# A transformer kernel on one core: seven products of zeros on TensorE at the start, and the splits of two weight blocks moved

## What is computed

```python
xn = _layernorm(x, axis=-1)
q = jnp.einsum('bsd,ed->bse', xn, Wq)
k = jnp.einsum('bsd,ed->bse', xn, Wk)
v = jnp.einsum('bsd,ed->bse', xn, Wv)
kvt = jnp.cumsum(k * v, axis=-2) * denom
vhat = q * kvt
x = x + jnp.einsum('bse,fe->bsf', vhat, Wo) + _L0_ffn_ref(xn, ...)
```

## Time and profile before

| | |
|---|---|
| three runs, us | 727.02, 727.24, 730.93 (median 727.24) |
| the profiled execution's own time, us | 730.96 |
| its span, us | 729.1 |
| mean granted clock of TensorE, share of full | 0.988 |
| TensorE matmuls busy | 667.8 us (92% of the span) |
| VectorE / ScalarE / GpSimd busy | 69% / 54% / 49% |

### The profile page before, as it was taken

How to read it: one execution, slowest core, us unless ns; L and a number is a source line. 1 busy time by engine, 2 the same in 40 slices (tenths; PEclk the granted TensorE clock), 3 DMA queues, 4 the chain that set the end, 5 groups by cost and what they waited for, 6 DMA issues and landing times.

```text
span 729.1 us, 13255 instructions
## 1 busy us (share of the span) xinstructions
PE 667.8 (92%) x4656; PEld 536.8 (74%) x4656; DVE 505.1 (69%) x964; ACT 395.1 (54%) x694; POOL 358.8 (49%) x299
## 2 busy tenths in 40 slices
PE   4998899899889899999899999989999989999996
PEld 4776676798878677776677777677777767777774
DVE  6978769568576748675867686585858486568645
ACT  3664325456455554754854482765475395448173
POOL 1346685766566533461646263454537162326453
PEclk9999899999999899999999999999999999999999
DMA  8437847697776577020025021004303000302100
GB/s 315 133 127 232 302 151 231 224 284 252 263 266 198 185 226 223 20 70 2 1 76 125 4 63 27 1 2 124 80 8 81 2 1 30 81 9 59 30 2 30
DMA packets 66804, 82.76 MB, mean 113 GB/s; under 512 B 7090, under 2 KB 50354, under 8 KB 66738
## 3 DMA queue, kind: packets, MB, share of 16 engines
q1 hardware_dynamic: 63156, 73.39, 31.8%
q0 software_dynamic: 3072, 8.39, 3.6%
q10 hardware_dynamic: 512, 0.13, 0.1%
HBM read 40.34 MB, written 28.84 MB: 95 GB/s over the span
## 4 chain that ended last, share of the span: by engine, by line
PE 52%; ACT 11%; DVE 11%; issue 10%; SPq 8%; DMA 4%; POOL 3%; ACTq 1%; POOLq 0%; DVEq 0%
PE acc L660 4%; SPq L623 4%; PE acc L662 4%; PE acc L661 4%; SPq L619 3%; PE pm L660 2%; PE pm L662 2%; PE ring L660 2%; PE pm L661 2%; PE ring L997 2%; PE ring L661 2%; PE ring L662 2%; PE pv L660 2%; POOL xs L1638 2%; ACT act L1490 2%
## 5 line engine op out<-in xcount | busy, mean ns | idle before, releaser
L1600 POOL TENSOR_TENSOR hl<-hf,hh 128x512 fp32r<-128x512 f32 (+1 forms) x76 | 100.5, 1322 | 230.1 <-ACT hh L1281 230.1
L1281 ACT ACTIVATE hh<-hf 128x512 fp32r<-128x512 f32 (+1 forms) x76 | 47.6, 629 | 75.4 <-DVE hf L2152 60.8
L660 PE MATMUL acc<-hh,wh 128*128 128x512 f32 (+1 forms) x168 | 70.4, 419 | 5.8 <-POOL hl L1600 5.8
L2216 DVE TENSOR_REDUCE mx<-ring 128x2 f32<-128x512 f32 (+1 forms) x96 | 61.6, 683 | 10.3 <-PE ring L999 10.3
L662 PE MATMUL acc<-hl,wh 128*128 128x512 f32 (+1 forms) x168 | 66.7, 397 | 0.0
L661 PE MATMUL acc<-hh,wl 128*128 128x512 f32 (+1 forms) x168 | 66.6, 396 | 0.0
L2152 DVE TENSOR_TENSOR hf<-hf,pv 128x512 f32<-128x512 f32 x64 | 43.6, 682 | 30.7 <-PE pv L662 29.3
L1739 POOL TENSOR_TENSOR pl<-act,ph 128x512 f16<-128x512 f32 x32 | 41.5, 1298 | 34.3 <-ACT ph L1495 31.4
L1472 ACT ACTIVATE hf<-pm 128x512 f32<-128x512 f32 x56 | 33.4, 596 | 44.6 <-PE pm L662 38.7
L1027 PE MATMUL ring<-qT,kT 98*128 98x256 bf16 (+1 forms) x256 | 43.8, 248 | 12.1 <-ACT act L1490 12.1
L660 PE MATMUL pv<-xh,wh 128*128 128x512 f32 x128 | 53.5, 418 | 0.0
(11 more groups left out here) (292 smaller groups left out, 2084.7 us busy)
## 6 DMA issues: line engine op xcount, KB each, us to landing
w4s<-w4hl SPq DMA_DIRECT2D x16, 512.0 KB, 4.2
ws<-qs SPq DMA_DIRECT2D x12, 512.0 KB, 5.2
qT<-qp SPq DMA_DIRECT2D x96, 64.0 KB
kT<-kp SPq DMA_DIRECT2D x96, 64.0 KB
xs<-yg SPq DMA_DIRECT2D x2, 2944.0 KB, 13.4
ys<-act SPq DMA_DIRECT2D x22, 256.0 KB, 3.7
stage<-w SPq DMA_DIRECT2D x8, 608.0 KB, 4.6
xh<-xs SPq DMA_DIRECT2D x12, 256.0 KB, 4.5
```

The source lines that it names most:

```text
L660: pe.matmul(o, w_hi, x_hi, start=first, stop=False, skip_group_check=True)
L1281: a.activation(h_parts(n)[0][0:rows, :], hf[0:rows, n % 2, :], ACT.Copy).then_inc(s_hh, 1)
L1600: return pool.tensor_tensor(dst, src, hi.bitcast(F32), ALU.subtract)
L2216: v.tensor_reduce(mx[:, i, h0:h0 + nh], ring[j % 2][:, :].rearrange("p (n k) -> p n k", n=nh), AX.X, ALU.max).then_inc(s_mx, 1)
```

## The change

TensorE gets seven products at the very start, after a wait for `s_zero`. Both operands are the zeroed tensor `yg`; each writes bank `ring[3]` (128 x 512), which nobody reads before `qkv(0,1,0)` overwrites it. On ScalarE the high parts of blocks 2 and 3 are made between `tokens_hi(0)` and `token_std(1)`; before, block 2 came behind `token_std(1)` and block 3 behind `v_scaled(0,1)`, together with block 4. GpSimd's and VectorE's own queues are as before; GpSimd's low part of block 3 waits for ScalarE's high part.

```diff
@@ constants
 EARLY, TURN_W = 13, 15
+WARM = 7
@@ TensorE
+            pe.wait_ge(s_zero, 1)
+            for _ in range(WARM):
+                pe.matmul(ring[3][:, :], yg[:, 0, 0:P], yg[:, :, :].rearrange("p a d -> p (a d)"), start=True, stop=True,
+                          skip_group_check=True)
             pe.wait_ge(s_ident, 16)
             turn_tokens(0)
@@ ScalarE
             token_std(0)
             weights(0, 1)
             tokens_hi(0)
+            weights(2, 3)
             token_std(1)
-            weights(2)
             for g in range(G):
                 v_scaled(g, 0)
                 if g < G - 1:
                     tokens_hi(g + 1)
                 v_scaled(g, 1)
                 if g == 0:
-                    weights(3, 4)
+                    weights(4)
```

## The result

| | before | after |
|---|---|---|
| median of 20 runs, us | 728.62 | 726.87 |
| lowest to highest, us | 725.68 to 732.38 | 722.53 to 730.12 |
| ratio to before, 95% interval | | 0.9969 (0.9954 to 0.9984) |
| span of the profiled execution, us | 729.1 | 723.3 |

The change makes the kernel faster by 0.31% of 728.6, 2.3 us, with 1.2 to 3.4 us in the interval; the medians differ by 1.75. The 0.5% of the prediction is not reached. The profiled executions differ by 5.8 us, more than the medians, so the span is no measure for the gain; what the rest is stands in "Why the prediction held".

A forecast was written before the change was run, and what follows sets the result against it. TensorE, busy 92% of the span, loses time at the start to the low clock and waits. VectorE's lead of 1.55 us, smaller than TensorE's 2.05, gives 727.24 - 1.55 = 725.7 us; range 723.4 to 729.6.

The forecast's parts named there:

- The smaller lead counts: After the first attention: of TensorE's lead of 2.05 us and VectorE's of 1.55, the gain is 1.55.
- The zeros: TensorE's start: seven zero products run from 1.35 us and end at 9.2, the clock rising after 3.7 us.
- What they delay: First tokens: transposes start 0.6 us later but run faster; `qkv(0,0,0)` stays at 11.2, its 18 products end at 15.4.
- GpSimd holds norm 1: Group 1's norm on VectorE: GpSimd's block 3 split, 12.9 to 15.3, makes it end at 16.4, 0.8 us later.
- The scans are freed: VectorE's scans in `attention(0,1)`: no longer held by GpSimd, they take 1.27 us and attention ends at 23.95, not 25.51.
- The whole gain is block 3's: At the start: moving block 3 brings the gain; the zeros bring about 0.2 us to VectorE's chain, nothing that decides.
- Rival 1: TensorE, 15.4 to 17.5: the clock falls without products, adding 1.7 us to the next ones; 727.1 us, chance 0.18.
- The rule against the zeros: TensorE, 9.2 to 11.2: transposes may not keep the clock up, so it may fall; sum the same within 0.5 us.
- Rival 2: TensorE's start: zeros outlast the tokens' arrival, each us beyond 9.2 delaying norm 1 by one; up to 729.9 us, chance 0.12.
- Rival 3: Group 1's norm: GpSimd's split does not hold it back, which returns 0.8 us; 724.9 us, chance 0.10.
- Rival 4: Later scans beside GpSimd's splits, as at 65.59: contention falls otherwise, sparing up to 5 us or adding waits; chance 0.08.
- Everything behind moves by it: Rest of the kernel: no event behind the start is fixed in time, so all of it moves by 1.55 us.

The follow-up runs named there:

- e11: The changed kernel run again without alteration, on a third chip; median 742.44 us, ratio to before 0.9963.
- e10: The changed kernel with two more zero products in front of group 2's last down projection; median 741.47 us, ratio to before 0.9952.
- e2: The changed kernel without its zero products, keeping the new ScalarE order; ratio to before 0.9978.
- e3: The changed kernel with block 3 loaded and its high part made ahead of block 2; ratio to before 0.9959.
- e1: The changed kernel with its zero products kept and ScalarE's order put back to that of before; ratio to before 0.9971.
- e6: The changed kernel with block 3 ahead of block 2 and five zero products in place of seven; median 727.82 us, ratio to before 0.9980.
- e7: The changed kernel with block 3 ahead of block 2 and no zero products; median 728.27 us, ratio to before 0.9997.
- e9: The changed kernel with block 3 first, five zeros at the start and two before group 2's last down projection; median 741.63 us, ratio to before 0.9969.
- e4: The changed kernel with fourteen zero products in place of seven; median 732.00 us, ratio to before 1.0044.
- e5: The changed kernel with GpSimd's low part of block 3 cut into four instructions; ratio to before 0.9992.

## Why the prediction held

- **Faster by 1.55 us on the path, within 0.5%: right in direction and size.** 1.71 at the landmark, 1.75 by the medians, 2.3 by the ratio. That the numbers lie so close is luck in part: two more executions of this start have leads of 1.29 (e11) and 1.01 (e10), since their zeros ended at 10.18 and 10.43.
- **"The smaller lead counts": the step that failed, though the sum came out.** The 1.55 was VectorE's lead at the end of `attention(0,1)`. That lead is 1.33 (25.51 against 24.18). TensorE's lead in front of `shared(0,0)` is 1.91 (23.75 against 21.84; 2.05 forecast), and it is TensorE whose work runs through from there to the end of the first down products (35.08 before). VectorE had time to spare before: its `gated(0)` was done at 28.81, and TensorE came to `shared(0,2)`, which waits for it, at 29.36. After, TensorE is there first and waits some 0.16 us for the end of `gated(0)` at 27.48. VectorE and TensorE, before and then after:

```profile
28.12 0.69 DVE L2019 TENSOR_TENSOR hf<-act,ring 128x512 f32<-128x512 f32 x1 [0.28 <-ACT act L1273]
29.36 0.40 PE L660 MATMUL ring<-xh,wh 128*96 128x512 f32 x1
```
```profile
26.79 0.69 DVE L2024 TENSOR_TENSOR hf<-act,ring 128x512 f32<-128x512 f32 x1 [0.28 <-ACT act L1278]
27.53 0.47 PE L661 MATMUL ring<-xh,wh 128*96 128x512 f32 x1
```

  So the lead at the landmark is TensorE's less a short wait, 1.83 at this place and 1.71 at 43.75. So VectorE's lead was forecast 0.22 us too large, and 0.5 us that it had to spare before stands in no term of the sum; the two errors have opposite signs, and the sum came out near 1.71. In e2 TensorE waits for nothing there, and its lead of 1.33 (29.36 against 28.03) is that of its landmark.
- **The zeros**: start 1.35 forecast, 1.31 measured; end 9.2 forecast, 9.48 in the profile after and 9.17 to 10.43 over seven profiled executions with seven zeros; the average, 9.8, is above the forecast. The price of 0.86 and 1.72 us from the earlier trace rows held: seven more took 6.2 us.
- **What they delay**: `qkv(0,0,0)` forecast at 11.2 by the landing of block 1, at 11.42 and released by VectorE's `tokens_lo(0)`, which the zeros delay (at 12.37 in e10); end of its 18 products 15.4 and 15.75.
- **ScalarE's two splits cost the root nothing**: they end at 13.09 (12.9 forecast), the root starts at 13.63 (13.6).
- **GpSimd holds norm 1**: 12.9 to 15.3 forecast, 13.16 to 15.59; the norm's end 16.4 and 16.71, that is GpSimd's end and 1.12, both. e3 shows that without this hold the landmark comes about 1 us sooner.
- **The scans are freed**: `attention(0,1)` ends at 23.49 + 0.69 = 24.18, 23.95 forecast, 25.51 before. No wait in front of `shared(0,0)`, at 21.84 (21.7).
- **"The whole gain is block 3's"**: right for the changed kernel's landmark (e2), too strong for the zeros, which alone lead by 0.6 us (e1), and by 1 to 2 in the order without the hold (e3 and e6 against e7). The leads are alternatives on one path and do not add.
- **Rival 1, the clock falls in the second pause**: not seen. In none of the ten profiled executions with zeros at the start are the products behind either pause 0.43 apart.
- **The rule against the zeros: no sign of it.** In the first pause TensorE runs no product from 9.48 to 11.42, and from 7.87 to 11.27 in e9, with the eight transposes in it, and the products behind are 0.23 apart in all ten. The Trainium skill (TensorE: Matmul & The Clock Gate, Part 4: PE-mode transpose), by which transposes do not count as busy time in the way of products, would have allowed a fall there; the measurement shows none.
- **Rival 2** was priced about rightly: 6.2 us more of zeros cost 5.95 at the landmark (e4), 0.70 and 0.95 us more cost 0.42 and 0.70 (e11, e10). **Rival 3**: 0.8 us forecast for a norm that is not held, 0.96 measured (e3). **Rival 4** named the routing scan at 65.59, 6.21 us: it takes 6.17 to 6.22 us in every kernel here, however the start was moved.
- **"Everything behind moves by it", and the reference for the time.** It holds to the first routing scan (65.59 before): the lead there is that of the landmark within 0.02 us in every kernel. Behind it, it does not hold. At TensorE's row of 99.80 e2's lead of 1.33 has shrunk to 0.55 (99.25), and e1's of 0.58 has grown to 0.96 (98.84). Between the profiles of before and after the lead grows, from 1.71 at the landmark to 2.32 at TensorE's row of 99.80 (after: 97.48) and 5.8 at the end. The change does not reach there; most of the growth goes with the clock, which fell at other places: 0.6 us of it arise near 80 us, 1.1 between 98 and 118 and 1.5 near 245, each where before was at the lower level and after was not. Behind the idle time of 1.76 us it fell before and did not after:

```profile
97.48 0.50 PE L661 MATMUL acc<-hh,wh 96*128 96x512 f32 x1 [1.76 <-POOL hl L1605]
```

The stretches around it, before and then after (columns: us, PE busy, PEld busy, DVE busy, ACT busy, POOL busy, granted clock, DMA share, GB/s):

```profile
60.00:120.00 60.00, 52.97 (x224) 41.80 (x223) 45.78 (x77) 19.32 (x31) 40.63 (x33) 0.91 0.75 251
...
240.00:720.00 480.00, 453.98 (x3460) 356.32 (x3459) 326.45 (x596) 276.31 (x460) 219.30 (x185) 0.99 0.20 58
```
```profile
60.00:120.00 60.00, 52.74 (x231) 41.56 (x230) 48.30 (x81) 20.33 (x32) 40.98 (x33) 0.97 0.75 261
...
240.00:720.00 480.00, 452.31 (x3468) 355.01 (x3466) 324.86 (x592) 275.11 (x458) 219.60 (x184) 1.00 0.20 56
```

The prediction had put its 3.7 us between two levels of the runs down to something the change does not touch, and had added it to its forecast for the profiled execution: 729.4, measured 725.1. With 20 runs of before there are no two levels but a spread of 7 us, and for the changed kernel it goes with the granted clock: of the changed kernel's runs, the six with a mean clock of 0.988 to 0.990 took 728.75 to 730.12 us, the fourteen with 0.991 to 0.997 took 722.53 to 727.60.

Open: why e1, with 0.6 us at the landmark, has a ratio as good as the changed kernel's (its interval begins at 0.9 us). One execution's landmark stands there for twelve; a zeros' end near 9.5 in the others would explain it, but was not measured. Why the leads of e5 and e6 do not reach the time of the runs is open too: before was profiled once, and what its landmark is on the two other chips, or in other executions, is not known.

## What to carry to other kernels

Where a split or a copy on one engine can hold another engine, moving it out of one wait moves it into the next: look at what VectorE does at the new place before counting the gain. Warm-up work on an idle TensorE is worth what the first products gain only if they are what the next step waits for, and it costs most of its overhang once it outlasts the data. Where two engines both get ahead, ask of each how much time it had to spare before: the smaller lead counts only if that engine had none. A gain of 0.2 to 0.3% at the start of a kernel is explained from an event near the change, in single profiles, and its size comes from many runs; the two need not agree, and one span against another can be off by more than the gain.

## What was not expected of the hardware

The same seven products, from the same start, ended between 9.17 and 10.43 us, since the clock rose at different times: the records of the zeros went from a distance of 0.85 us to one of 0.43 at about 4.5 us in e5 and at about 7.1 in e10. An idle time of 1.76 us was followed by the lower level in the profile of before and not in that of the changed kernel, while 1.9 us without any product but with eight transposes (3.4 us in e9) was not in any of ten executions. A VectorE instruction that GpSimd held ended 0.15 us behind the end of GpSimd's instruction, in the changed kernel and twice in e5. And chips differ: on one, before took 745.12 us in the median and the changed kernel 742.44, with about the same ratio (0.9963). The start is not what differs there (landmark 44.17); against the changed kernel's other profile e11 falls back by 10 us between 130 and 150 us, where its DMA share is 0.58 in place of 0.87 and its granted clock 0.83 in place of 1.00. Why is open.
